# Second quantised layer begins right behind its fourth tile, a second half's second lane runs three steps behind its first, dt with zero rows

## What is computed

```python
x = x + _L0_attn_a_ref(_layernorm(x), Wqkv, Wproj)      # causal attention, 16 heads of 16, rotary
x = x + _L0_ffn_ref(_layernorm(x), weight, bias)        # quantised 256x256 layer
x = x + _L0_attn_b_ref(_layernorm(x), ...)              # mamba mixer (512 inner, 16 states) and MLP
x = x + _L0_ffn_ref(_layernorm(x), weight, bias)        # the same quantised layer again
```

## Time and profile before

| | us |
|---|---|
| median of three runs | 9594.14 |
| the profiled execution, whole | 9585.67 |
| its span, first to last instruction | 9583.9 |
| TensorE busy | 7974.4 (83%) |
| VectorE busy | 7554.9 (79%) |
| GpSimd busy | 4327.9 (45%) |
| ScalarE busy | 4256.5 (44%) |
| mean granted TensorE clock | 0.937 of full |

### The profile page before, as it was taken

How to read it: one execution, slowest core, us unless ns; L and a number is a source line. 1 busy time by engine, 2 the same in 40 slices (tenths; PEclk the granted TensorE clock), 3 DMA queues, 4 the chain that set the end, 5 groups by cost and what they waited for, 6 DMA issues and landing times. The chain is left out here.

```text
span 9583.9 us, 101363 instructions
## 1 busy us (share of the span) xinstructions
PE 7974.4 (83%) x33332; PEld 3981.1 (42%) x33332; DVE 7554.9 (79%) x11589; ACT 4256.5 (44%) x7991; POOL 4327.9 (45%) x2631
## 2 busy tenths in 40 slices
PE   5788797887978878788887888878888797887978
PEld 2344353443434434344343444434344353443534
DVE  5787977879687796877878778787787977879777
ACT  2534535254442644525435354353534535345353
POOL 1451825518254272642726336273461724618255
PEclk8998999989999999999989999899999999989999
DMA  3020020200202002020020200102011020100202
GB/s 80 1 48 7 5 50 1 54 1 5 50 1 54 1 9 46 0 54 1 13 42 0 54 1 21 34 0 54 1 28 27 0 54 1 40 15 1 53 1 53
DMA packets 265207, 230.19 MB, mean 24 GB/s; under 512 B 26947, under 2 KB 237635, under 8 KB 264531
## 3 DMA queue, kind: packets, MB, share of 16 engines
q1 hardware_dynamic: 264678, 223.50, 10.8%
HBM read 151.60 MB, written 70.25 MB: 23 GB/s over the span
## 5 line engine op out<-in xcount | busy, mean ns | idle before, releaser
L639 POOL TENSOR_TENSOR arena<-arena 128x1024 f32<-128x1024 f32 x1024 | 2434.8, 2388 | 1204.4 <-DVE arena L1042 797.8
L779 ACT ACTIVATE PS<-arena,Aneg 128x512 f32<-128x512 f32 x2048 | 1411.4, 691 | 1624.5 <-DVE XNT L1082 887.9
L705 ACT ACTIVATE arena<-PS 128x512 f32<-128x512 f32 (+3 forms) x3072 | 1287.0, 507 | 869.5 <-PE PS L1258 864.6
L949 DVE TENSOR_REDUCE pm<-PS 128x1 f32<-128x512 f32 (+3 forms) x1728 | 1051.3, 663 | 281.1 <-PE PS L1237 178.8
L1379 PE MATMUL PS<-XNT,identf 128*128 128x512 f32 x2048 | 1010.8, 618 | 310.1 <-POOL XNT L622 310.1
L601 POOL TENSOR_SCALAR_AFFINE_SELECT arena<-arena 128x512 f32<-128x512 f32 x512 | 328.1, 641 | 2044.7 <-ACT arena L705 2044.7
L1234 PE MATMUL PS<-arena 96*128 96x512 bf16 (+3 forms) x3072 | 1101.2, 383 | 120.5 <-PEq L1453 41.4
L1379 PE MATMUL PS<-arena,identf 128*128 128x512 f32 x2048 | 1004.8, 614 | 161.9 <-DVE arena L1058 161.9
L1258 PE MATMUL PS<-arena 99*128 99x512 bf16 (+3 forms) x3072 | 892.4, 332 | 5.9
L1364 PE MATMUL PS<-arena,sel 96*128 96x512 bf16 x1664 | 505.2, 385 | 373.8 <-DVE arena L1058 303.9
L687 ACT ACTIVATE XNT<-PS 128x512 f32<-128x512 f32 x320 | 186.6, 597 | 1313.9 <-PE PS L1185 1312.4
(11 more groups left out here) (145 smaller groups left out, 13391.9 us busy)
## 6 DMA issues: line engine op xcount, KB each, us to landing
pieces_scratch<-arena SPq DMA_DIRECT2D x816, 64.0 KB
arena<-pieces_scratch SPq DMA_DIRECT2D x68, 384.0 KB, 10.2
arena<-pieces_scratch SPq DMA_DIRECT2D x85, 256.0 KB, 10.6
arena<-in_x SPq DMA_DIRECT2D x17, 1024.0 KB, 5.7
U<-in_x SPq DMA_DIRECT2D x17, 1024.0 KB, 5.6
arena<-pieces_scratch SPq DMA_DIRECT2D x136, 128.0 KB, 9.6
out<-X SPq DMA_DIRECT2D x64, 256.0 KB, 5.9
arena<-pieces_scratch SPq DMA_DIRECT2D x17, 768.0 KB
```

Of the source, the lines that this page charges most:

```text
L639: nc.gpsimd.tensor_tensor(DB[:, n % 2], DTU[:, j, half(th)].unsqueeze(1).to_broadcast([P, SP2, TH]), BB[:, SP2 * sg:SP2 * (sg + 1), :], AL ...
L705: A(PT[s % len(PT)][:, hh, 0:w], bank(t_bank(n))[:, 0:w], ACT.Exp, scale=DH ** -0.5)\
L779: A(bank(da_bank(m)), DT[:, j, half(th)], ACT.Exp, scale=Aneg[:, j, SP2 * sg + ss:SP2 * sg + ss + 1]).then_inc(S("dA"), 1)
L949: V_.tensor_reduce(out=dst, in_=bank(r % 3)[:, 0:share * w].rearrange("p (h w) -> p h w", h=share), op=ALU.max, axis=AX.X, negate=True).th ...
```

## The change

Four things change.

First, the second quantised layer. The statistics of tile 3 are taken at the fourth tile instead of the fifth, and the centring is cut into two tiles per pair: pair 0 at `n == NMLP - 5`, pair 1 at `NMLP - 4`.

Second, `quantize` is rewritten with one generator for each lane and a `skew`: in a second half (of both quantised layers, since `pairs[0]` is not 0) lane 1 starts three steps behind lane 0, so the first three and the last three steps stand alone.

Third, `DTR` and `dtw` get 128 rows, of which 112 are zero, and the dt product contracts over all 128. POOL writes the zeros ahead of the loads in the preamble, once.

Fourth, to make room, `sel` keeps one column of each 128, and PE reads it with a step of 0.

```diff
-        dtw = sb("dtw", [DR, DI])
+        dtw = sb("dtw", [P, DI])
...
-        sel = sb("sel", [3 * 2 * DS, 2 * DS, P], BF16)
+        sel = sb("sel", [3 * 2 * DS, 2 * DS], BF16)
+
+        DTR = sb("DTR", [P, T])
...
-        DTR = view(16400, T)
...
+        STEPS = 10
+
+        SKEW = 3
...
+        def quantize(own, rows, lanes, skew=0):
+
+
+            nb = rows // QB
+            running = [lane_steps(own, nb, *lane) for lane in lanes]
+            for step in range(STEPS + skew * (len(lanes) - 1)):
+                for n, lane in enumerate(running):
+                    if 0 <= step - skew * n < STEPS:
+                        ins = next(lane)
+                        if step - skew * n == STEPS - 1:
+                            yield ins
...
+                sp.wait_ge(pre["zero"], 2)
...
-                nc.vector.tensor_copy(sel[:, :, :], stage[0:3 * 2 * DS])
+                nc.vector.tensor_copy(sel[:, :], stage[0:3 * 2 * DS, :, 0])
...
+            @block.gpsimd
+            def _(pool):
+                nc.gpsimd.memset(dtw[:, :], 0.0).then_inc(pre["zero"], 1)
+                nc.gpsimd.memset(DTR[:, :], 0.0).then_inc(pre["zero"], 1)
...
-                         quant_place(f, n, 0)) for n in pairs]):
+                         quant_place(f, n, 0)) for n in pairs], SKEW if pairs[0] else 0):
...
-                    if i:
+                    if i and i != NT // NTH:
                         tile_stats(2, i - 1)
+                    if i == NT // NTH - 1:
+                        tile_stats(2, i)
                 if n in FRONT_AT:
                     vector_front(dve, FRONT_AT.index(n))
 
-                if n == NMLP - 4:
-                    centre(0, lambda i: quant_rows(1, i // 2)[:, i % 2, :])
-                    dve.wait_ge(S("xn"), NT * 2 + NT // NTH)
-                if n in (NMLP - 4, NMLP - 3):
-                    grid(1, [n - (NMLP - 4)])
+                if n in (NMLP - 5, NMLP - 4):
+                    p = n - (NMLP - 5)
+                    centre(range(2 * p, 2 * p + 2), lambda i: quant_rows(1, i // 2)[:, i % 2, :])
+                    dve.wait_ge(S("xn"), NT * 2 + 2 * p + 2)
+                    grid(1, [p])
...
-                MM(bank(DT_BANK[n]), dtw[:, tile(j)], DTR[0:DR, half(th)], start=True, stop=True)\
+                MM(bank(DT_BANK[n]), dtw[:, tile(j)], DTR[:, half(th)], start=True, stop=True)\
                     .then_inc(S("dtp"), 1)
+            def selector(s):
+                return sel[:, s:s + 1].to_broadcast([3 * 2 * DS, P])
...
-                            ins = MM(bank(c_bank(ss)), sel[:, DS + SP2 * sg + ss, :], BCP[:, half(th)],
+                            ins = MM(bank(c_bank(ss)), selector(DS + SP2 * sg + ss), BCP[:, half(th)],
```

More of the change, by code:

```diff
@@ L238, in build, with lane_steps @@
                  (cosT[:, :, :], cos_in), (sinT[:, :, :], sin_in)]
-        def quantize(own, rows, lanes):
-            nb = rows // QB
-            at = [own.n] * len(lanes)
+        TS, STT, TT = nc.vector.tensor_scalar, nc.vector.scalar_tensor_tensor, nc.vector.tensor_tensor
+        STEPS = 10
+        SKEW = 3
+        def lane_steps(own, nb, scl, rcp, amx, v, h, a, src):
             def blocks(t):
                 return t.rearrange("p (n q) -> p n q", q=QB)
[L250 to L277, removed]
@@ new lines, in lane_steps @@
+            at = own.did(nc.vector.tensor_reduce(out=amx, in_=blocks(src), op=ALU.max, axis=AX.X,
+                                                 apply_absolute_value=True))
+            yield
+            own.wait(at)
+            at = own.did(TS(scl, amx, 1.0 / 7.5, 1e-30, ALU.mult, ALU.max))
+            yield
+            own.wait(at)
+            at = own.did(nc.vector.reciprocal(rcp, scl))
+            yield
+            own.wait(at)
+            at = own.did(TT(blocks(v), blocks(src), rcp.unsqueeze(2).to_broadcast([P, nb, QB]), ALU.mult))
@@ new lines, in lane_steps @@
+            yield
+            own.wait(at)
+            at = own.did(TS(h.bitcast(U32), v.bitcast(U32), 0x7F800000, None, ALU.bitwise_and))
+            yield
+            own.wait(at)
+            at = own.did(TS(h, h, 1.0, 1.0 / 16, ALU.max, ALU.mult))
+            yield
+            own.wait(at)
+            at = own.did(STT(out=a, in0=h, scalar=ROUND, in1=v, op0=ALU.mult, op1=ALU.add))
+            yield
+            own.wait(at)
+            at = own.did(STT(out=src, in0=h, scalar=ROUND + 2, in1=v, op0=ALU.mult, op1=ALU.add))
@@ new lines, in lane_steps @@
+            yield
+            own.wait(at)
+            at = own.did(STT(out=a, in0=src, scalar=ONE_STEP_DOWN, in1=a, op0=ALU.mult, op1=ALU.min))
+            yield
+            own.wait(at)
+            yield STT(out=v, in0=h, scalar=-ROUND, in1=a, op0=ALU.mult, op1=ALU.add)
+        def quantize(own, rows, lanes, skew=0):
[7 more added lines that the diff above has]
+                            yield ins
```

12 lines of the change are left out of this document (6 added, 6 removed).

## The result

The changed kernel takes 9601.31 us, the median of 12 runs (9591.27 to 9642.14), beside 9592.14 us for the kernel before (12 runs): a ratio of 1.0016, 95% interval 1.0009 to 1.0024. That is 0.57 us a pass slower by the two medians and 0.96 by the ratio. The forecast was no change, 9594. The time lies in the range, but the change is slower, with an interval that lies above 1, though single runs of the two kernels overlap. The profiled execution (9595.14 us) is one of the faster ones: in the traces the passes are only 0.35 us further apart than before (590.87 against 590.52 us), and what follows accounts for that.

The account below looks back on a forecast made before the run. No engine is full; stages bound the kernel, DVE setting each pass's end. Terms −1.8 + 1.55 + 1.5 − 1.1 = +0.15 us a pass gave 9596; with attention absorbing, the forecast was no change, 9594, range 9538 to 9630.

Parts of the forecast that it names:

- first half of the second layer: Pair 0 moves into DVE's 2.69 us wait for the fifth `w2` tile; less contention with POOL, −1.8 us a pass.
- order of steps, second layer: Skewed second half: lone DVE steps end later and POOL's L591 blocks them; upper end taken, +1.25 us a pass.
- order of steps, first layer: Same skew in the first layer's second half; lower end taken, without blocking by L591, +0.3 us a pass.
- clock behind the skew, second layer: PE's clock falls in the gap before the last turn, slowing it and 16 `rows` products; +1.5 us a pass.
- the same, first layer: PE's clock behind the skew costs nothing in the first layer, since it has already fallen there.
- dt stage: Full 128 rows hold PE's clock through the dt products and shorten ACT's softplus wait; −1.1 us a pass.
- attention and border: Attention swallows or turns round changes of about 1 us in a pass's tail, so no change was forecast.
- Both collisions: Pair 1's L261 beside POOL's bias loses up to 1.96 us; L264 or another step beside L591 loses 0.74.
- The slack of the next front: SP's stack comes about 3.1 us later, covered by 6.67 us of slack before SP's output; no cost.
- the rival that the clock would fall anyway: At the dt products the clock falls despite 128 rows, losing the 1.1 us a pass gain; 9614 us, chance 0.07.
- The absorption: A late pass had shorter attention, 143.60 against 145.22 us, so about 1 us of tail change can vanish there.
- The selector: One column of `sel` read with step 0: load unchanged at 98 ns, counted 0; rival at twice that 9619, chance 0.05.

Follow-up runs that it names:

- experiment 3: Changed kernel with SKEW = 0 and 16 rows in the dt product, leaving the early first half: 9571.01 us, ratio 0.9981 to the kernel before.
- experiment 7: Kernel before, with three more 384 KB DMA transfers that SP issues ahead of the output: 9609.86 us, ratio 1.0008 to the kernel before.
- experiment 9: Changed kernel with SKEW = 0, plus ten dummy products in PE's preamble, loop untouched: 9536.93 us, ratio 0.9944 to the kernel before.
- experiment 5: Changed kernel, skew kept, with five dummy products on PE between the two lanes' turns: 9574.03 us, ratio 0.9968 to the kernel before.
- experiment 2: Changed kernel with 16 dt rows and the old place of the first half, skew kept: 9689.77 us, ratio 1.0105 to the kernel before.

## Why the prediction was wrong, step by step

The terms of the sum beside what the traces show, in us a pass:

| term | forecast | measured |
|---|---|---|
| first half of the second layer | −1.8 | −2.08 |
| order of steps, second layer | +1.25 | +1.16 |
| order of steps, first layer | +0.3 | +1.16 |
| clock behind the skew, second layer | +1.5 | +1.03 |
| the same, first layer | 0 | −0.21 |
| rewritten `quantize`, tail | not seen | −0.15 |
| dt stage | −1.1 | −1.15 |
| head of the scans | not seen | +0.55 |
| attention and border | absorb | +0.03 |
| sum | +0.15, forecast as 0 | +0.34 |

**First half of the second layer: right.** −1.8 forecast, −2.08 measured in every pass. Of that 0.13 is something I missed in the diff: the old `quantize` made its first step wait for DVE's instruction before it, the new one doesn't. With the first half in its old place the new `quantize` gives 21.50 instead of 21.63, and 0.15 in the tail; that it is this wait is read from the code, no run takes it alone out. Both collisions came out at the figures taken, 2.50 and 1.16 us. L267 to L279 of pair 1 did not stretch (0.43 and 0.69 us).

**The slack of the next front: wrong, though not in this kernel.** I let 6.67 us of SP's slack cover the later stack. It is issued 3.0 us later behind tile 3 (3.1 forecast), and it did not delay SP or attention's data. But PE's code comes through queues too: in experiment 3 its packet ends 2.2 to 3.3 us behind the last sum at all 15 borders, and half of the gain is lost there. That more data in the queues delays this packet is shown by experiment 7, and that its place is what costs by experiment 9; whether the later stack or the earlier end of the tail brings the two together is not told apart. In the changed kernel the longer tail hides it (border 4.11).

**The skew's order of steps: right in the second layer, too low in the first.** 1.25 in the second layer, measured 1.16. In the first I took the lower end, +0.3, with no row that told the two layers apart, and it is 1.16 there too (experiment 5). The half clock in the first layer of the kernel before, 1.31 us in every pass, hides most of it from a plain comparison: 50.22 with that half clock stands beside 50.07 without it. The stall beside L611 is 0.73 us in one step (1.42 against 0.69), in both layers. That is as the rule of the Trainium skill on two-input instructions has it (SBUF — State Buffer, section "Who interferes with whom"), and both layers near their upper end is what the prediction drew from that rule.

**The clock behind the skew: right in kind, too high in size.** I wrote "+1.5 in the second layer, nothing in the first". In the second layer the mean is 1.03, since the clock falls in 10 of 16 passes and not in all. PE stands idle there for 0.2 to 0.7 us and, behind one turn, for 2.47 us, not about 5. In the first layer half clock costs 1.10 us on the mean, from nothing in five passes to 2.2 in three, where before it cost 1.31 in all; against the kernel before that is −0.21, so "nothing" was near. Alone, the skew makes it worse: in experiment 2 the first layer is at 52.30, 2.23 above full clock.

**dt: right in its place, half given back.** −1.15 in the stage against −1.1, and the rival that the clock would fall anyway is refuted. But I looked for no half clock further on. It fell on the six dummies ahead of the spread of B, +0.55 over the passes of the changed kernel.

**The absorption: the step that decided the forecast, and it failed.** I took one late pass with a short attention (143.60 us) as a rule. In the kernel before all five passes that began late are like that (143.36 to 143.60), the others take 145.2 to 145.4, and the long ones have a further 3.4 us at half clock at their end. But it is not the lateness that does it: in experiment 7 every border is late, and only nine of the 15 attentions behind them are short. In the changed kernel 15 of 16 take 145.2 to 145.4, and attention is 0.47 us longer on the mean, not shorter; the border is 0.44 shorter, and the two absorb nothing. L672 (L652 before) stands 590.96 us apart instead of 590.51.

So the steps that failed are the absorption, for which I overruled a sum of +0.15 that had the sign, the order of steps in the first layer (+0.3 for 1.16) and the head of the scans (nothing for +0.55). That the sum came within 0.2 of the traces is luck: the two terms that were too low, by 1.41 together, were met by the clock in the second layer (0.47 too high), the front (0.28 more than forecast), the first layer's clock and the rewritten `quantize`. And the traces' +0.35 is that of one execution each; the medians say 0.57 and the ratio 0.96.

The selector (98 ns before and after) and the preamble cost nothing that shows.

Not settled: why PE's clock falls at different places in neighbouring passes of the same loop, and so why one execution of the changed kernel takes 9591 us and two of twelve take 9640.

## What to carry to other kernels

Where an engine's clock depends on its work, two lanes that were together are worth more than their overlap: pull them apart and the matrix engine stands idle twice. Price such a change by the products behind the gap, at half clock, in every place where it occurs, and fill the gap before judging the idea. Compare a stage only with passes at the same clock: a half clock that was there before can hide a price of the same size, as the 1.16 us in the first layer were hidden here. A gain at the end of a loop's pass must also be followed over the border: the next pass's code has to be there, and dummy products placed to hold the clock are a cost when the clock has fallen already.

## What the hardware showed that I had not expected

PE's first instruction of a pass came 3.2 to 3.6 us behind DVE's last sum when its code packet was there, and 1.5 to 2.1 us behind the packet's end when it was late. Forty PE instructions in the preamble moved that packet by some 16 us and were worth 0.22% by the ratios (0.9966 to 0.9944) in a kernel whose loop is unchanged.

One skew, without a single instruction more, cost 6.3 us a pass in one kernel and, in the changed kernel against the one without it, 0.50% or 3.0 us by the ratios and 2.06 by the traces.
